# Moving layer-norm moments of three batches and two raw weight loads from the start of the feed-forward into the tail and start of the attention before it

## What is computed

```python
# x: (4, 1024, 256), ctx_1024: (4, 154, 256)
x = x + tanh(g_xattn[1]) * L1_xattn(layernorm(x), ctx_1024)        # 16 heads of 16, causal, 154 keys
x = x + tanh(g_ffn[1]) * L1_ffn(layernorm(x), w1, conv_w, conv_b, w2)

def L1_ffn(x, w1, conv_w, conv_b, w2):      # w1: (1024, 256), w2: (256, 1024)
    h = bit_linear(x, w1)                   # per-row 8-bit values of x, ternary w1 (scale: mean of |w1|)
    h = depthwise_conv1d(h, conv_w, conv_b) # three taps along the tokens
    return bit_linear(silu(h), w2)
```

## Time and profile before

| | |
|---|---|
| Median of three runs | 3335.99 us (3334.81 to 3341.94) |
| The profiled execution | 3334.0 us, span 3332.3 us |
| TensorE, VectorE, ScalarE, GpSimd busy | 93%, 74%, 49%, 23% of the span |
| Mean granted clock of TensorE | 0.977 of full speed |
| Second attention | from about 2634.6 to 3102.8 us of the span |
| Feed-forward | from about 3103.1 us to the end |

### The profile page before, as it was taken

How to read it: one execution, slowest core, us unless ns; L and a number is a source line. 1 busy time by engine, 2 the same in 40 slices (tenths; PEclk the granted TensorE clock), 3 DMA queues, 4 the chain that set the end, 5 groups by cost and what they waited for, 6 DMA issues and landing times. The chain is left out here.

```text
span 3332.3 us, 63809 instructions
## 1 busy us (share of the span) xinstructions
PE 3115.2 (93%) x20868; PEld 2889.6 (87%) x20868; DVE 2462.3 (74%) x4864; ACT 1646.7 (49%) x3133; POOL 758.3 (23%) x1370
## 2 busy tenths in 40 slices
PE   4999999999999999999899899999999879999588
PEld 3999999999999999999788788898999778888476
DVE  5777777777777777878767677787787756666787
ACT  2555555555555555555444322222222256666587
POOL 2222222223222232222011121111111123332120
PEclk9999999999999999999999999999999989999799
DMA  3000000000000000000200323323233200000000
GB/s 93 16 14 11 12 14 12 11 14 9 17 12 12 12 11 14 11 9 3 57 5 5 83 88 94 103 92 108 93 93 92 65 1 1 0 0 0 26 20 32
DMA packets 117168, 113.94 MB, mean 34 GB/s; under 512 B 39535, under 2 KB 82856, under 8 KB 116904
## 3 DMA queue, kind: packets, MB, share of 16 engines
q1 hardware_dynamic: 116904, 110.62, 11.4%
HBM read 105.33 MB, written 5.24 MB: 33 GB/s over the span
## 5 line engine op out<-in xcount | busy, mean ns | idle before, releaser
L448 ACT ACTIVATE x_pth<-x_ps 128x512 fp32r<-128x512 f32 (+1 forms) x768 | 376.3, 528 | 253.4 <-PE x_ps L713 250.8
L1067 ACT ACTIVATE moe_sil<-moe_ps,moe_b 128x512 f32<-128x512 f32 x256 | 176.4, 689 | 574.0 <-PE moe_ps L1233 548.3
L553 DVE TENSOR_TENSOR x_ptl<-x_ps,x_pth 128x512 fp32r<-128x512 f32 (+1 forms) x768 | 402.6, 551 | 30.8 <-ACT x_pth L448 18.3
L468 ACT ACTIVATE all_buf<-all_buf,x_nmx 128x1178 f32<-128x1178 f32 x256 | 327.6, 1280 | 130.8 <-DVE all_buf L588 130.5
L1258 PE MATMUL moe_ps<-moe_w2z,moe_gh 128*128 128x256 f32 (+1 forms) x1280 | 371.4, 290 | 19.9 <-DVE moe_gl L1190 19.8
L588 DVE TENSOR_SCALAR_CACHE_REDUCE all_buf<-x_ps 128x1182 f32<-128x1182 f32 x256 | 354.4, 1384 | 24.1 <-PE x_ps L724 14.4
L713 PE MATMUL x_ps<-ident,all_buf 128*128 128x128 f32 x2560 | 365.7, 274 | 2.1 <-DVE x_ptl L553 1.8
L1258 PE MATMUL moe_ps<-moe_w2z,moe_gl 128*128 128x256 f32 x1280 | 364.5, 285 | 0.0
L1258 PE MATMUL moe_ps<-moe_w2l,moe_gh 128*128 128x256 f32 x1280 | 364.3, 285 | 0.0
L739 PE MATMUL x_ps<-x_pth,x_vh 128*128 128x256 f32 x1152 | 346.3, 301 | 0.0
L739 PE MATMUL x_ps<-x_pth,x_vl 128*128 128x256 f32 x1152 | 325.7, 283 | 0.0
(11 more groups left out here) (373 smaller groups left out, 8155.1 us busy)
## 6 DMA issues: line engine op xcount, KB each, us to landing
moe_gate<-moe_cw_rows SPq DMA_DIRECT2D x512, 128.0 KB, 2.9
all_buf<-in_L_ffn_w_dram SPq DMA_DIRECT2D x6, 1024.0 KB, 8.9
xres<-in_x_dram SPq DMA_DIRECT2D x4, 1024.0 KB, 8.8
x_rawv<-in_L_xattn_Wkv_dram SPq DMA_DIRECT2D x16, 256.0 KB, 2.7
x_rawk<-in_L_xattn_Wkv_dram SPq DMA_DIRECT2D x32, 128.0 KB, 2.1
x_rawq<-in_L_xattn_Wq_dram SPq DMA_DIRECT2D x32, 128.0 KB, 2.2
x_rawo<-in_L_xattn_Wo_dram SPq DMA_DIRECT2D x32, 128.0 KB, 2.0
all_buf<-in_L_ffn_w_dram SPq DMA_DIRECT2D x8, 512.0 KB, 5.3
```

What stands on the lines that cost most here:

```text
L448: act.activation(turn_dst(pth, x, lo, hi), turn_src(x, g), ACT.Copy).then_inc(hi_done, 1)
L468: act.activation(p[:, w % 4, DUP:DUP + R_KV], p[:, w % 4, DUP:DUP + R_KV], ACT.Exp, bias=nmx[:, w % 2:w % 2 + 1], scale=-1.0, accum_out=su ...
L553: last = dve.tensor_tensor(turn_dst(ptl, x, lo, mid), turn_src(x, g)[:, 0:mid - lo, :], turn_dst(pth, x, lo, mid).bitcast(F32), ALU.subtract)
L1067: act.activation(dst[:, q % 2, :], ps[:, HID + q % 2, :], ACT.Silu, bias=bias).then_inc(silu_done, 1)
```

## The change

The raw weights w1 and w2 are loaded by SP at the start of the second attention, behind that stage's own seven loads, with a semaphore that both stages share. In steps 10 to 17 of the last batch VectorE makes the moments of three tiles per step, for batches 0 to 2 (24 tiles); in step 18 it adds epsilon, in step 19 ScalarE takes the root, in step 21 VectorE refines it. The results go to tensors shared by the stages. In the feed-forward only `nmr` is left at the start, the moments of batch 3 stay in slot 3 and their root in slots 5 and 6, and slot 2 has no moments. In step 10 and step 14 the moments stand ahead of the projection's addition (L1722).

```diff
@@ ctx_attention_stage
+        next_st, next_mv, next_var, next_root, next_rstd = S.st, S.mv, S.var, S.root, S.rstd
+        NROOT = 2
...
+        NEXT, DONE = LOOP, 3 * TPB
+        NEXT_VAR = NEXT + DONE // 3
...
             sp.dma_start(bor[:, :], A["L1_xattn_bo"].rearrange("(a d) -> a d", a=1)).then_inc(d_in, 16)
+            load_ffn_weights(sp, A, S)
...
+                if not after and w == NEXT_VAR + 1:
+                    act.wait_ge(stats, NROOT)
+                    act.activation(next_root[:, 0:DONE], next_var[:, 0:DONE], ACT.Sqrt).then_inc(rooted, 1)
...
+            def next_moments(tiles):
+                dve.wait_ge(x_added, CPB + CPB * (BATCH - 1))
+                for t in tiles:
+                    own.step(dve.bn_stats(next_st[:, t % TPB, :], xres[:, t, :]))
+                own.wait()
+                for t in tiles:
+                    own.step(dve.bn_aggr(next_mv[:, t, :], next_st[:, t % TPB, :]))
...
                     normalise(CPB * b + (w + 6) // 4)
+                if not after and NEXT <= w < NEXT_VAR:
+                    next_moments(range(3 * (w - NEXT), 3 * (w - NEXT + 1)))
+                if not after and w == NEXT_VAR:
+                    own.wait()
+                    dve.tensor_scalar(next_var[:, 0:DONE], next_mv[:, 0:DONE, 1], EPS, None, ALU.add).then_inc(stats, 1)
+                if not after and w == NEXT_VAR + 3:
+                    dve.wait_ge(rooted, NROOT)
+                    newton_rsqrt(own, dve, next_var[:, 0:DONE], next_root[:, 0:DONE], next_rstd[:, 0:DONE])
                 c = behind(w, PROJECT + 1, 4, before)
@@ new, ahead of ffn_stage
+def load_ffn_weights(sp, A, S):
+    w1, w2 = ffn_raw(S)
+    sp.dma_start(w1, A["L1_ffn_w1"].rearrange("(b p) d -> p b d", p=P)).then_inc(S.ffn_w, 16)
+    sp.dma_start(w2, A["L1_ffn_w2"].rearrange("(k p) h -> p k h", p=P)).then_inc(S.ffn_w, 16)
@@ ffn_stage
-            sp.dma_start(w1[:, :, :], A["L1_ffn_w1"].rearrange("(b p) d -> p b d", p=P)).then_inc(d_w1, 16)
...
-            sp.dma_start(w2[:, :, :], A["L1_ffn_w2"].rearrange("(k p) h -> p k h", p=P)).then_inc(d_w, 16)
...
-                    pool.wait_ge(rstd_made, 1 + b // 2)
+                    pool.wait_ge(rstd_made, 1 + b // 3)
...
-            act.wait_ge(stats, 1)
-            act.activation(root[:, 0:2 * TPB], var[:, 0:2 * TPB], ACT.Sqrt).then_inc(rooted, 1)
             act.wait_ge(set_up, 4)
-            act.wait_ge(d_w1, 16)
+            act.wait_ge(S.ffn_w, 32)
...
-            act.wait_ge(d_w, 48)
+            act.wait_ge(d_w, 32)
...
+            def offsets(lo, hi):
                 dve.scalar_tensor_tensor(nmr[:, lo:hi], mv[:, lo:hi, 0], -1.0, rstd[:, lo:hi], ALU.mult, ALU.mult).then_inc(rstd_made, 1)
...
-            moments(0, TPB)
-            moments(TPB, 2 * TPB)
-            variances(0, 2 * TPB)
-            rstds(0, 2 * TPB, 1)
+            offsets(0, LAST)
...
-                if s in (2, 3):
-                    moments(s * TPB, (s + 1) * TPB)
                 if s == 3:
-                    variances(2 * TPB, 4 * TPB)
+                    moments()
...
```

More of the change, by code:

```diff
@@ L1921, in ffn_stage @@
         ones = sb("ones", [P, P])
-        st, mv = sb("st", [P, TILES, 6]), sb("mv", [P, TILES, 2])
-        var, root, rstd, nmr = (sb(n, [P, TILES]) for n in ("var", "root", "rstd", "nmr"))
+        st, mv, var, root, rstd = S.st, S.mv, S.var, S.root, S.rstd
+        nmr = sb("nmr", [P, TILES])
+        LAST = TILES - TPB
         y = sb("y", [P, TPB, DIM])
@@ L1955, in chunk_dst @@
             return t[:, b % 2, k, h * CH:(h + 1) * CH]
-        d_w1, d_w, set_up, dve_own, pool_own = (sem(n) for n in ("d_w1", "d_w", "set_up", "dve_own", "pool_own"))
+        d_w, set_up, dve_own, pool_own = (sem(n) for n in ("d_w", "set_up", "dve_own", "pool_own"))
         stats, rooted, rstd_made = sem("stats"), sem("rooted"), sem("rstd_made")
@@ L2089, in _ @@
                 if s == 5:
-                    act.wait_ge(stats, 2)
-                    act.activation(root[:, 2 * TPB:], var[:, 2 * TPB:], ACT.Sqrt).then_inc(rooted, 1)
+                    act.wait_ge(stats, 1)
+                    act.activation(root[:, LAST:], var[:, LAST:], ACT.Sqrt).then_inc(rooted, 1)
                 if s == 6:
@@ L2105, in _, with moments @@
             own = Chain(dve, dve_own)
-            def moments(lo, hi):
-                for t in range(lo, hi):
-                    own.step(dve.bn_stats(st[:, t, :], xres[:, t, :]))
+            def moments():
+                for t in range(LAST, TILES):
+                    own.step(dve.bn_stats(st[:, t - LAST, :], xres[:, t, :]))
                 own.wait()
-                for t in range(lo, hi):
-                    own.step(dve.bn_aggr(mv[:, t, :], st[:, t, :]))
+                for t in range(LAST, TILES):
+                    own.step(dve.bn_aggr(mv[:, t, :], st[:, t - LAST, :]))
                 own.wait()
-            def variances(lo, hi):
-                own.wait()
-                dve.tensor_scalar(var[:, lo:hi], mv[:, lo:hi, 1], EPS, None, ALU.add).then_inc(stats, 1)
-            def rstds(lo, hi, k):
-                dve.wait_ge(rooted, k)
-                newton_rsqrt(own, dve, var[:, lo:hi], root[:, lo:hi], rstd[:, lo:hi])
-                own.wait()
+                dve.tensor_scalar(var[:, LAST:], mv[:, LAST:, 1], EPS, None, ALU.add).then_inc(stats, 1)
+            def offsets(lo, hi):
                 dve.scalar_tensor_tensor(nmr[:, lo:hi], mv[:, lo:hi, 0], -1.0, rstd[:, lo:hi], ALU.mult, ALU.mult).then_inc(rstd_made, 1)
@@ L2221, in _ @@
                 if s == 6:
-                    rstds(2 * TPB, 4 * TPB, 2)
+                    dve.wait_ge(rooted, 1)
+                    newton_rsqrt(own, dve, var[:, LAST:], root[:, LAST:], rstd[:, LAST:])
+                    own.wait()
+                    offsets(LAST, TILES)
             for n in range(TILES - TPB, TILES):
@@ L2354 @@
     moe_w: object
+    ffn_w: object
 def flamingo_program(nc, A, out):
@@ L2366, in flamingo_program @@
                    st=sb("st", [P, TPB, 6]), mv=sb("mv", [P, TILES, 2]), var=sb("var", [P, TILES]),
-                   root=sb("root", [P, TILES]), rstd=sb("rstd", [P, TILES]), moe_w=nc.alloc_semaphore("all_moe_w"))
+                   root=sb("root", [P, TILES]), rstd=sb("rstd", [P, TILES]), moe_w=nc.alloc_semaphore("all_moe_w"), ffn_w=nc.alloc_semaphore("all_ffn_w"))
         ident_set = nc.alloc_semaphore("ident_set")
```

8 lines of the change are left out of this document (5 added, 3 removed).

## The result

The kernel before took 3336.67 us (median of 5 executions, 3334.81 to 3341.94), the changed one 3323.14 us (5 executions, 3320.97 to 3323.99): ratio 0.9955, 95% interval 0.9942 to 0.9968, or 13.5 us where 9.4 were forecast. It is faster by over 0.2%, as forecast. The forecast ratio, 3326.6 / 3336.0 = 0.9972, lies just outside the interval, and 13.5 us is more than the 13.0 us (3336.0 - 3323.0) at the end of the stated range. The profiled execution of the changed kernel took 3322.19 us, against 3334.0 before.

What follows compares the result with a forecast made beforehand. The prediction took the serial moments at the feed-forward's entry and in slot 2 as path. Its terms, 8.59 + 0.93 - 0.1 - 0 = 9.4 us, took 3336.0 to 3326.6 us, range 3323.0 to 3331.5.

Steps and rivals of the forecast that it cites:

- The entry: Feed-forward's start: without moments and root, VectorE's normalising follows `nmr` directly and starts 8.59 us sooner.
- The worth of the loads: Feed-forward's entry: with the weight loads left there, the sum of |w1| would wait and give back nearly 5 us.
- Slot 2: Feed-forward: removing batch 2's moments gives 0.93 us of their 3.4, since `low` waits for ScalarE's `high`.
- The rival that slot 2 gives all 3.4: Feed-forward: `high` does not set the pace, so 3.4 us come instead of 0.93, total 3324.1; chance 8%.
- The tail: Attention steps 10 to 21: moments of 1.33 us per step hide in VectorE's idle times; cost 0.1 us, unhidden 10.6.
- a tail that absorbs only part: Rival, attention's tail: steps 10, 11, 12 and 14 cost 1.33 us each, 5.3 in all, total 3331.9; chance 8%.
- The rival of the falling clock: Attention's tail: pushed maxima give TensorE gaps, its clock falls and costs 19.8 us, total 3346.4; chance 4%.
- The loads at the attention's start: Attention's start: w1 and w2, issued behind seven earlier loads and served in order, cost 0 us.
- a sign of an error: Attention's start: TensorE's first wait should stay 10.2 us; that wait grown would show the prediction wrong.
- shared queues: Rival, attention's start: the loads share bandwidth and delay TensorE by 2.7 to 5.5 us, total 3329.3 to 3332.1; chance 10%.
- TensorE's clock: Feed-forward's entry: the shorter idle still leaves the lower level, so no change, at most 1.0 us to either side.
- the measurement's scatter of 1 to 2 us: Whole kernel's time: the assumed scatter of measured times, used in setting the forecast's range.

Runs made afterwards that it cites:

- e1: The changed kernel unaltered, run again with more executions: 3326.92 us, ratio 0.9972 to the kernel before.
- e11: The changed kernel unaltered, run a third time: 3327.41 us, ratio 0.9973 to the kernel before.
- e5: The changed kernel with ScalarE's scaling of w2 moved from slot 2 to slot 3: 3324.28 us, ratio 0.9967 to the kernel before.
- e9: The changed kernel with batch 0 also normalised and both weight sums taken in the attention's tail, w2 scaled in slot 2: 3323.06 us, ratio 0.9965.
- e6: The changed kernel with batch 0 normalised and both weight sums taken in the attention's tail, and w2 scaled in slot 3: 3324.03 us, ratio 0.9963.
- e8: The changed kernel with the loads of w1 and w2 held back until VectorE normalised the attention's first rows: 3326.69 us, ratio 0.9971.
- e7: The changed kernel with each step's three moments made twice in steps 10 to 17: 3334.9 us, ratio 0.9996 to the kernel before.
- e3: The kernel before with only the two weight loads moved, the moments left in the feed-forward: 3334.91 us, ratio 0.9995.

## Why the prediction was right, and where it was wrong

- **The entry** was forecast at 8.59 us and measured at 8.58, and everything behind it that the text named holds: `nmr` first, the sum of |w1| done before the first scales, the table load out of the way.
- **The worth of the loads** was put at nearly 5 us, and is 3.5. The step that failed is the reading of 3110.43 as the end of the load. It was the end of the wait for the root; the load alone is through 6.1 us behind the barrier. The sum was not touched, since it has the loads moved.
- **Slot 2** was forecast at 0.93, limited by `high`, with an idle of some 2.4 us ahead of `low`. Measured: idle 2.40; slot 4's product to slot 5's 5.47 us instead of 6.40, 0.93 less (0.77 and 0.79 less in e1 and e11); e5 shows that `high` was the limit. The rival that slot 2 gives all 3.4 is out.
- **The tail** was forecast at 0.1 and costs nothing: 47.4 to 47.9 us in the kernels before and after and in e1 to e5 and e9 to e11, with e6 and e8 above that by the clock in the last two projections. The slack has an end: e7, with 1.46 us more per step, pays up to 8.6 of 11.7. So a tail that absorbs only part, the rival with its limit of 1.4 us, is what doubled insertions bring, though the limit itself was not measured. The rival of the falling clock did not come in the change (1.00 over the insertions); with the doubled ones one short stretch at the lower level did.
- **The loads at the attention's start** were forecast at 0. TensorE's wait was 11.0 us instead of 10.2, which I had named as a sign of an error. Over thirteen profiles it is 0.6 us in the mean, and it is gone 32 instructions later. The served-in-order reading of the earlier trace rows holds to that size: 2.7 or 5.5 us, as for shared queues, never showed. By the Trainium skill (DMA: Bandwidth & Descriptors, Latency and other measured facts), whose 0.2 us on average and 2 us at high load gave an estimate of 1.8, a loaded memory could have put the last landing later. The traces agree with the sign and with at most 1.5 of it, and disagree on the end of the sum: the difference is gone before it could lower the gain to 7.6. The executions alone could not have told 7.6 from 9.4 (e1's interval is 6.3 to 12.3 us).
- **TensorE's clock** at the entry was taken at no change, within 1.0 us. From the first turn of the rows to the first product it took 8.29 us before and 7.80 after, 0.5 less. Since the other kernels show 7.38 to 8.12 with this or the old entry (7.38 in e3, which has the old one), this is scatter.

**The sum of 9.4 stands**: 9.3 us in e1 and 9.0 in e11 by their ratios, and 10.3 in the profiled pair's feed-forward: 8.58 + 0.93, 0.5 at the entry's turning and 0.3 further on.

**The step that failed is the last one**, the measurement's scatter of 1 to 2 us. The range (3323.0 to 3331.5, a gain of 4.5 to 13.0) rested on it in part, and no run shows it: the three executions at hand then lay 7.1 us apart already (3334.81 to 3341.94). In its place the runs showed this: single executions of the kernel before ran from 3329.93 to 3342.43 us over the 66 of the three groups, 12.5 us apart, and 20 of the change from 3321.61 to 3331.20. Medians of five executions each gave 13.5 us, 11 and 33 gave 10.0, 9 and 13 gave 9.4. The mechanism and its terms were right; the scatter was mis-sized.

The traces show no missed term for the 4 us by which the first measurement exceeds the sum. The changed feed-forward took 216.18 us in that measurement's profile and 216.21 and 216.28 in e1 and e11, whereas the stretch ahead of step 10, whose code is the same in all kernels but for the two loads and a memset, ended anywhere from 3049.3 to 3060.6 us in the thirteen profiles. Whether the 4 us were chance alone stays open. All five executions of the first measurement took 3323.99 us or less, as only five of the later 20 did; five independent draws from the later ones would do that about once in a thousand times. So something that differs from one session to another may have played a part, and no run here tells what.

## What to carry to other kernels

A stage's serial start, here 8.7 us of one engine while the others stand, is worth moving into the finishing steps of the stage before, where that engine has known holes: price one insertion, hold it against the smallest hole, and stop there, because a second copy is path for the greater part (up to 8.6 of 11.7 us). Before a load is moved with the work that covers it, find out which of them ends last, from the idle time ahead of the row itself (5.89 us, for VectorE) and not from the row's start. And where single executions lie 10 us apart, a change of 9 needs tens of them, or the distance between the same two instructions in two traces. With one profile each that gave 10.3 us for a sum of 9.4; over five profiles of the same feed-forward it scattered by 1.8 us, so a term under 1 us needs several profiles or a shorter distance.

## What the runs showed of the hardware

**The scatter goes with TensorE's clock.** The mean granted clock of each execution goes with its time. For the kernel before, over the 66 executions of the three groups:

| mean granted clock | executions | median, us |
|---|---|---|
| 0.973 | 1 | 3341.6 |
| 0.974 | 5 | 3339.2 |
| 0.975 | 19 | 3338.7 |
| 0.976 | 17 | 3336.5 |
| 0.977 | 12 | 3334.7 |
| 0.978 | 11 | 3331.8 |
| 0.979 | 1 | 3329.9 |

In the traces these are short stretches at the lower level (1.2 GHz) inside work that otherwise runs at the full one (2.4 GHz). Many stand at the same place in both kernels' profiles, others in one alone: in the second attention the kernel before had them at 2744, 2795, 2822 and 2873 us, the changed one at 2688, 2948 and 3026. The kernel's code there is the same. At six of these (all but 2688) TensorE falls 1.6 us behind the other profile within the stretch, and makes good up to 1.0 us of it in the 15 us behind it. What sets off such a stretch no run here shows.

**A lower level costs by its place.** The last two projections of the attention, from their first piece to their last, took 4.25 us in e6 and 4.26 in e8 instead of the changed kernel's 3.42, because TensorE's clock was at the lower level from their start, behind a wait of 2.5 to 2.8 us, and not only from their middle. In e7 TensorE waits more often: the granted clock stayed at 1.00 over 22 us in which it was busy for 18.10 (20.32 in the change), and was at 0.50 from 3099.60 to 3103.00, behind 4 us (3095 to 3099) in which it was busy for 2.34.
